# Two RoPE multiplications and one subtraction of the token mix moved from VectorE to GpSimd in an attention and channel-mix kernel

## The reference

```python
q = x @ Wq + bq;  k = x @ Wk + bk;  v = x @ Wv + bv      # split into 16 heads of 64
q = q * cos_pos + rotate_half_interleaved(q) * sin_pos   # RoPE
k = k * cos_pos + rotate_half_interleaved(k) * sin_pos
ctx = softmax(q @ k.T / 8) @ v
x = layernorm(x + ctx)

x_prev = x shifted by one token (zero at the first)
xr = mu_r * x + (1 - mu_r) * x_prev
xk = mu_k * x + (1 - mu_k) * x_prev
r = sigmoid(xr @ W_r.T)
out = layernorm(x + r * (square(relu(xk @ W_k.T)) @ W_v.T))
```

## Time and profile before

| | us |
|---|---|
| timed runs (2) | 4389.8 and 4480.0, median 4434.9 |
| profiled execution | 4356.1 |
| its span (slowest core, 7) | 4354.5 |
| spans of the eight cores | 4334.8 to 4354.5 |
| PE busy | 3102 (71%) |
| ACT busy | 2453 (56%) |
| DVE busy | 1065 (24%) |
| POOL busy | 245 (6%) |

### The profile page before, as it was taken

One profiled execution on the slowest core, in us unless ns is written; L12 is line 12 of the kernel. 1 busy time (PEld: TensorE's weight loads), 2 busy tenths in 40 slices (PEclk: granted clock), 3 DMA queues, 4 the chain that ended last, 5 costly groups with the idle time before them and its releaser, 6 DMA issues.

```text
span 4354.5 us, 53551 instructions; the slowest of 8 cores (4334.8 to 4354.5 us)
## 1 busy us (share of the span) xinstructions
PE 3102.2 (71%) x19520; PEld 1154.2 (27%) x19520; DVE 1065.3 (24%) x2489; ACT 2452.9 (56%) x2333; POOL 245.4 (6%) x260
## 2 busy tenths in 40 slices
PE   1555678878887888788788878887888787115554
PEld 1222222222222222322222222222223222002222
DVE  2222522212221221222122212212221000045553
ACT  0444057757775777577667757775776888001111
POOL 0111100010000001000100010010001000100000
PEclk9677899989998999899899989998998899557778
DMA  7342421111111110211011111102110000331110
GB/s 219 146 164 106 155 78 49 49 40 49 49 39 58 50 49 20 69 59 49 22 68 49 39 50 49 59 20 69 49 49 17 5 1 1 93 110 37 35 57 39
DMA packets 80352, 262.80 MB, mean 60 GB/s; under 512 B 6242, under 2 KB 40290, under 8 KB 61410
## 3 DMA queue, kind: packets, MB, share of 16 engines
q1 hardware_dynamic: 77282, 242.59, 16.5%
q0 software_dynamic: 2816, 16.78, 1.0%
HBM read 225.27 MB, written 34.08 MB: 60 GB/s over the span
## 4 chain that ended last, share of the span: by engine, by line
PE 44%; ACT 26%; issue 6%; DVE 6%; DMA 4%; DVEq 2%; POOL 1%; ACTq 0%; SPq 0%; POOLq 0%
ACT pt_sb L773 25%; PE ps_c L758 14%; PE ps_stB L747 6%; PE ps_b L560 5%; PE ps_b L599 5%; PE ps_stA L747 4%; PE ps_d L1261 1%; PE ps_d L1235 1%; PE ps_c L866 1%; PE ps_b L663 1%; DMA xf_b<-xT_spill 1%; DVE ctxT_f L791 1%; DVEq L168 1%; PE ps_b L921 1%; PE ps_c L798 1%
## 5 line engine op out<-in xcount | busy, mean ns | idle before, releaser
L773 ACT ACTIVATE pt_sb<-ps_stA,mhat_sb 128x1024 bf16<-128x1024 f32 x1024 | 1139.2, 1113 | 421.7 <-PE ps_c L758 258.0
L773 ACT ACTIVATE pt_sb<-ps_stB,mhat_sb 128x1024 bf16<-128x1024 f32 x1024 | 1139.9, 1113 | 270.2 <-PE ps_c L758 246.2
L758 PE MATMUL ps_c<-pt_sb,v_aug 128*65 128x512 bf16 x3968 | 1240.3, 394 | 0.0
L747 PE MATMUL ps_stB<-qT,kT 64*64 64x512 bf16 x4096 | 428.5, 404 | 186.1 <-ACT pt_sb L773 179.8
L747 PE MATMUL ps_stA<-qT,kT 64*64 64x512 bf16 x4096 | 430.6, 406 | 141.7 <-ACT pt_sb L773 126.5
L758 PEld LDWEIGHTS ps_c<-pt_sb,v_aug 128*65 128x65 bf16 x3968 | 279.5, 110 | 456.4 <-issue 456.4
L747 PEld LDWEIGHTS ps_stB<-qT,kT 64*64 64x64 bf16 x4096 | 136.4, 104 | 606.6 <-issue 600.8
L747 PEld LDWEIGHTS ps_stA<-qT,kT 64*64 64x64 bf16 x4096 | 135.9, 104 | 579.6 <-issue 572.4
L560 PE MATMUL ps_b<-xf_b,wkv_sb 128*128 128x512 bf16 x896 | 232.9, 407 | 51.1 <-DMA xf_b<-xT_spill 51.1
L654 POOL TENSOR_TENSOR ksq<-kT 128x512 bf16<-128x512 bf16 x112 | 115.4, 1037 | 2384.6 <-DVE kT L590 2370.5
L1156 PE MATMUL ps_t<-ident_sb,ctxg 128*128 128x128 f32 x136 | 33.0, 423 | 296.6 <-DVE ctxg L1146 296.6
(11 more groups left out here) (140 smaller groups left out, 2104.9 us busy)
## 6 DMA issues: line engine op xcount, KB each, us to landing
xf_b<-xT_spill SPq DMA_DIRECT2D x128, 1024.0 KB, 4.8
xst_f<-x_full SPq DMA_DIRECT2D x16, 2048.0 KB, 8.1
xT_spill<-xfT_st POOLq DMA_DIRECT2D x16, 1024.0 KB, 4.3
ctx_spill<-ctx_hp SPq DMA_DIRECT2D x8, 1088.0 KB, 5.8
xo_c<-x_own SPq DMA_DIRECT2D x17, 512.0 KB, 4.0
ctxg<-ctx_spill SPq DMA_DIRECT2D x17, 512.0 KB, 3.5
xst_f<-x_own SPq DMA_DIRECT2D x4, 2048.0 KB, 10.4
out<-xo_c SPq DMA_DIRECT2D x16, 512.0 KB, 2.6
```

Of the source, the lines that this page charges most:

```text
L747: r = e.matmul(ps_st[g].rearrange("p (b n) -> p b n", b=2) [half * 64:half * 64 + 64, h, 0:qn], kT2[buf][h * 64:h * 64 + 64, c * 128 + hal ...
L758: r = e.matmul(ps_c[h][0:65, 0:qn], v_aug[buf].rearrange("p (k x) -> p k x", k=KC) [:, cp, h * 65:h * 65 + 65], pt_sb[:, (cp % 4) * 1024 + ...
L773: sB.op("scalar", lambda e, g=g, c=c, hp=hp: e.activation(pt_sb[:, (c % 4) * 1024:(c % 4) * 1024 + 1024], ps_st[g][:, 0:1024], AF.Exp, bia ...
```

## The change

- Q RoPE: the two multiplications (`t1_sb`, `t2_sb`) go from DVE to POOL, without a drain between them. The addition into `qT2` stays on DVE as an operation of its own.
- K RoPE, in the fillers and in the prologue of head 0: the same with `bt1`, `bt2` and `kT2`. The list of a K/V tile in the fillers grows from ten items to eleven, so there are 194 items for 178.
- Token mix: mu * x + (1 - mu) * x_prev becomes x_prev + mu * (x - x_prev). POOL computes the difference of a chunk once (f32, into `tmp_f` or `tmp_g` in turn), DVE makes xr and xk from it by one scalar_tensor_tensor each. Sixteen tensor_scalar of a mix are gone from DVE and eight tensor_tensor come to POOL. xr and xk are now made chunk by chunk beside each other and no longer all of xr first.

```diff
-                def rope_q(e, pp=pp, hp=hp, qoff=qoff, qn=qn):
+                def rope_mul(e, pp=pp, qoff=qoff, qn=qn):
                     e.tensor_tensor(t1_sb[:, 0:qn], rq_sb[pp % 2][:, 0:qn],
                                     sinq_sb[:, qoff:qoff + qn], ALU.mult)
-                    e.drain()
-                    e.tensor_tensor(t2_sb[:, 0:qn], qpre[pp][:, 0:qn],
-                                    cosq_sb[:, qoff:qoff + qn], ALU.mult)
-                    e.drain()
-                    r = e.tensor_tensor(
-                        qT2[:, hp * FPAD + qoff:hp * FPAD + qoff + qn],
-                        t1_sb[:, 0:qn], t2_sb[:, 0:qn], ALU.add)
+                    r = e.tensor_tensor(t2_sb[:, 0:qn], qpre[pp][:, 0:qn],
+                                        cosq_sb[:, qoff:qoff + qn], ALU.mult)
                     return r
-                sA.op("vector", rope_q,
+                sA.op("gpsimd", rope_mul,
                       reads=[trk(f"rq{pp % 2}"), trk(f"qpre{pp}"), T["c_cosq"],
                              T["c_sinq"]],
-                      writes=[trk("qT2"), trk("t12")])
+                      writes=[trk("t12")])
+                sA.op("vector", lambda e, pp=pp, hp=hp, qoff=qoff, qn=qn:
+                      e.tensor_tensor(
+                          qT2[:, hp * FPAD + qoff:hp * FPAD + qoff + qn],
+                          t1_sb[:, 0:qn], t2_sb[:, 0:qn], ALU.add),
+                      reads=[trk("t12")], writes=[trk("qT2")])
...
-        def ropek(e, pp=pp, buf=buf, kt=kt):
+        def ropek_mul(e, pp=pp, kt=kt):
             e.tensor_tensor(bt1[:, :], rk_sb[pp][:, :],
                             sin2_sb[:, kt * 512:(kt + 1) * 512], ALU.mult)
-            e.drain()
-            e.tensor_tensor(bt2[:, :], kpre_sb[pp][:, :],
-                            cos2_sb[:, kt * 512:(kt + 1) * 512], ALU.mult)
-            e.drain()
-            r = e.tensor_tensor(kT2[buf][:, kt * 512:(kt + 1) * 512],
-                                bt1[:, :], bt2[:, :], ALU.add)
+            r = e.tensor_tensor(bt2[:, :], kpre_sb[pp][:, :],
+                                cos2_sb[:, kt * 512:(kt + 1) * 512], ALU.mult)
             return r
-        fl.append(lambda: sB.op("vector", ropek,
+        fl.append(lambda: sB.op("gpsimd", ropek_mul,
             reads=[trk(f"rk{pp}"), trk(f"kpre{pp}"), trk("cos2"), trk("sin2")],
-            writes=[trk(f"kT2_{buf}"), trk("btx")]))
+            writes=[trk("btx")]))
+        fl.append(lambda: sB.op("vector", lambda e, buf=buf, kt=kt:
+            e.tensor_tensor(kT2[buf][:, kt * 512:(kt + 1) * 512],
+                            bt1[:, :], bt2[:, :], ALU.add),
+            reads=[trk("btx")], writes=[trk(f"kT2_{buf}")]))
...
-            tags = ["dma", "kproj", "kevac", "rkmm", "rkevac", "rope",
+            tags = ["dma", "kproj", "kevac", "rkmm", "rkevac", "rope", "rope",
                     "vproj", "vevac", "vtr", "vsplit"]
...
-            def mix(e, doff=doff, dn=dn, tmp=tmp, mu=mu, om=om, dst=dst):
...
-                    e.tensor_scalar(tmp[:, 0:dn], cur, mu[:, cc:cc + 1],
-                                    None, ALU.mult)
-                    e.drain()
-                    r = e.scalar_tensor_tensor(
-                        dst[:, cc * 512:cc * 512 + dn], prv, om[:, cc:cc + 1],
-                        tmp[:, 0:dn], ALU.mult, ALU.add)
-                    e.drain()
...
+            sC.op("gpsimd", lambda e, dbuf=dbuf, dn=dn, cur=cur, prv=prv:
+                  e.tensor_tensor(dbuf[:, 0:dn], cur, prv, ALU.subtract),
+                  reads=xtags, writes=[trk(f"dmix{db}")])
+
+            def stt2(e, dbuf=dbuf, dn=dn, cc=cc, jb=jb, prv=prv):
+                e.scalar_tensor_tensor(
+                    xr_sb[jb][:, cc * 512:cc * 512 + dn], dbuf[:, 0:dn],
+                    mur_sb[:, cc:cc + 1], prv, ALU.mult, ALU.add)
+                r = e.scalar_tensor_tensor(
+                    xk_sb[jb][:, cc * 512:cc * 512 + dn], dbuf[:, 0:dn],
+                    muk_sb[:, cc:cc + 1], prv, ALU.mult, ALU.add)
+                return r
```

More of the change, by code:

```diff
@@ L962, in kv0_prologue, with ropek_mul @@
                 reads=[trk("b6")], writes=[trk(f"rk{pp}")])
-            def ropek(e, pp=pp, kt=kt):
+            def ropek_mul(e, pp=pp, kt=kt):
                 e.tensor_tensor(bt1[:, :], rk_sb[pp][:, :],
                                 sin2_sb[:, kt * 512:(kt + 1) * 512], ALU.mult)
-                e.drain()
-                e.tensor_tensor(bt2[:, :], kpre_sb[pp][:, :],
-                                cos2_sb[:, kt * 512:(kt + 1) * 512], ALU.mult)
-                e.drain()
-                r = e.tensor_tensor(kT2[0][:, kt * 512:(kt + 1) * 512],
-                                    bt1[:, :], bt2[:, :], ALU.add)
+                r = e.tensor_tensor(bt2[:, :], kpre_sb[pp][:, :],
+                                    cos2_sb[:, kt * 512:(kt + 1) * 512],
+                                    ALU.mult)
                 return r
-            sB.op("vector", ropek,
+            sB.op("gpsimd", ropek_mul,
                   reads=[trk(f"rk{pp}"), trk(f"kpre{pp}"), trk("cos2"),
                          trk("sin2")],
-                  writes=[trk("kT2_0"), trk("btx")])
+                  writes=[trk("btx")])
+            sB.op("vector", lambda e, kt=kt: e.tensor_tensor(
+                kT2[0][:, kt * 512:(kt + 1) * 512],
+                bt1[:, :], bt2[:, :], ALU.add),
+                reads=[trk("btx")], writes=[trk("kT2_0")])
             sB.op("gpsimd", lambda e, kt=kt: e.tensor_tensor(
@@ L1178, in emit_mix @@
         jb = j % 2
-        for eng, tmp, mu, om, dst, tag in (
-                ("vector", tmp_f, mur_sb, omr_sb, xr_sb[jb], f"xr{jb}"),
-                ("vector", tmp_g, muk_sb, omk_sb, xk_sb[jb], f"xk{jb}")):
-            def mix(e, doff=doff, dn=dn, tmp=tmp, mu=mu, om=om, dst=dst):
[L1183 to L1190, removed]
-                    e.tensor_scalar(tmp[:, 0:dn], cur, mu[:, cc:cc + 1],
-                                    None, ALU.mult)
-                    e.drain()
-                    r = e.scalar_tensor_tensor(
-                        dst[:, cc * 512:cc * 512 + dn], prv, om[:, cc:cc + 1],
-                        tmp[:, 0:dn], ALU.mult, ALU.add)
-                    e.drain()
-                return r
[L1199 to L1204, removed]
@@ new lines, in emit_mix @@
+        lo = (doff - 1) // 128
+        hi = (doff + dn - 1) // 128
+        xtags = [trk(f"x1T_{s}") for s in range(lo, hi + 1)]
+        for cc in range(NCC):
+            db = cc % 2
+            dbuf = (tmp_f, tmp_g)[db]
+            cur = x1T.rearrange("p (c t) -> p c t", c=NCC)[:, cc,
+                                                          doff:doff + dn]
+            prv = x1T.rearrange("p (c t) -> p c t", c=NCC)[:, cc,
+                                                          doff - 1:
+                                                          doff - 1 + dn]
+            sC.op("gpsimd", lambda e, dbuf=dbuf, dn=dn, cur=cur, prv=prv:
[8 more added lines that the diff above has]
+                    muk_sb[:, cc:cc + 1], prv, ALU.mult, ALU.add)
+                return r
+            sC.op("vector", stt2,
+                  reads=[trk(f"dmix{db}"), T["c_mur"], T["c_muk"]] + xtags,
+                  writes=[trk(f"xr{jb}"), trk(f"xk{jb}")])
```

## The result

The changed kernel is slower: the ratio of its time to that of the kernel before is 1.015, with a 95% interval of 1.010 to 1.020. On a time of 4356 us that is 66 us (44 to 88), where the sum had said 62.

A forecast was written before the change was run, and what follows sets the result against it. PE and ACT were busiest in attention; the Q stage was a serial chain with PE waiting at psa_u. 46 + 8 + 10 + 0 - 2 = +62 us, added to the fastest and median baselines, gave 4475 us midway, range 4405 to 4545.

The forecast's parts named there:

- the sum: Whole kernel: the predicted costs and gains of all parts added together, +62 us.
- the likeliest case: Whole kernel: time within 2% (88 us) of the kernel before, chance 0.78.
- Q RoPE, 46 us: Q stage, 40 tiles: longer DVE-POOL chain before PE's psa_u matmul, uncovered, costs 46 us, bounds 42 and 52.
- The clock, 8 us: Q stage: longer waits lower PE's granted clock, costing 8 us, bounds 0 and 39.
- Rival (a): Q stage: PE falls to the low clock throughout, 39 us for 8, sum +93, about 4506 us; chance 0.15.
- K/V of head 0, 10 us: First head's K/V stage, 16 tiles: DVE waits for POOL's multiplications, costing 10 us, bounds 5 and 16.
- Attention, 0 us: K RoPE under attention, 112 tiles: idle DVE and POOL time absorbs it, cost 0, bounds -10 and +20.
- the sign of being wrong: Changed profile: PE's wait growing by under 1 us, or attention moving by more than 20 us.
- rival (b): Attention: new filler spacing costs each projection burst 0.2 us more, 45 us, sum +107, about 4520 us; chance 0.08.
- The mix, -2 us: Token mix 0: subtractions on POOL and DVE work exclude each other, gaining 2 us, bounds -9 and +6.
- rival c: Token mix: POOL and DVE overlap freely, -9 us, sum +55, 4468 us; chance 0.05.
- Rival (d): Attention: DVE's shorter queue frees PE earlier, 112 us won, sum -50, about 4385 us; chance 0.02.

The follow-up runs named there:

- one_item: Changed kernel with the K RoPE's two POOL multiplications and DVE addition as one filler item, ten again; profiled time 4414.7 us, attention 3131.4 us.
- mix_dve: Kernel before with only the token mix's new formula, its difference also computed on DVE; profiled time 4394.1 us, first transposition to first projection of block C 81.7 us.

## Why the prediction was right, and where not

The direction and the likeliest case (within 2% of the kernel before, which had a chance of 0.78) came out as forecast, though the interval of 1.010 to 1.020 reaches to that bound. The agreement in the size is in part luck: +62 us in the sum, +66 by the ratio, but +80 between the fastest executions and on cores 0 to 3 of the two profiles, and the 18 us between are near the one wrong term. The time of 4475 us was put midway between two readings of a baseline that itself scattered from 4353 to 4592; the measured median of 4541 is 4 us inside the range given, and no term of the sum put it there. By its steps:

- **Q RoPE, 46 us.** Right: 45.5 us of wait, alone and in the whole change (43.0 on the 32 large tiles, for 42.6 in the sum, and 2.4 on the 8 small ones, for 3.7), and 13 us are left when PE has cover. One assumption in it was off. The multiplications were priced by the row of the squares, 1.035 us, and take 1.145; the hand-overs were in return shorter than put in, so the chain was 4.33 us for 4.24. The ratio of about 2 between the engines in the Trainium skill (GPSIMD Engine Reference, Engine selection), by which 33 us had been estimated, doesn't fit this trace: 1.145 against 0.425 us is 2.7.
- **The clock, 8 us.** Right in size: the stage grew by 6 to 10 us beside the wait. Over the Q projections on core 0 PE was busy for 183.0 us, for 172.1 before, at a mean granted clock of 0.68 for 0.70. Rival (a), 39 us, didn't come.
- **K/V of head 0, 10 us.** Right: 9.4. A round of DVE is 5.62 us (additions at 514.33 and 519.95) for 5.39 before; 5.75 had been predicted.
- **Attention, 0 us.** Wrong: 22 us, just above the upper bound of 20, which the prediction had also named as the sign of being wrong. The argument on POOL and DVE was right, as one_item shows: with 224 multiplications on POOL attention is as before. What failed was the last sentence of that step, that at 14.4 slots a tile for 14.2 "the items stay spread". The mean distance wasn't the question. The fillers are counted anew at each query tile's start, and the eleventh item moved the first projection of tiles 2 to 4 out of the pause at chunk 2. This is near rival (b), which had a cost by spacing, 45 us by a guess of 0.2 us a burst; it was given 0.08, and the mechanism in it, bursts meeting other PE work, is not the one found. Working out which item falls to which chunk from 0.703 and 0.766, as was done for the last items of each tile, would have shown it for the first ones.
- **The mix, -2 us.** -3.8 to -4.3. A subtraction beside DVE's work takes 1.60 us for 1.03, and the 9 us of free overlap (rival c) are not there. This is what the Trainium skill (SBUF — State Buffer, Who interferes with whom) says of such a pair of instructions, and the trace agrees. The term was some 2 us too small because six of the subtractions cost DVE 0.78 us each (1.53 for 0.75) and one 0.64, not 1.04. The squares of L1250 weren't held up (1.04 us each, for 1.07 before). The prediction credits the second engine with a gain that the formula alone gives: with everything on DVE it is the same.
- **Rival (d)** has no support: the wait list of attention has none of PE's K or V projections waiting for DVE, and freeing 0.8 us of DVE's time on each of 112 tiles moved nothing (one_item). Its 4385 us was counted from the median of 4434.9 and not from the base of the 4475.

## What to carry to other kernels

An operation moved to an idle engine is cheap where something else covers it and costs its full difference, hand-overs included, where the engine at the end has nothing else in its queue; so look first at what stands next in that queue, and move the waiting instruction later before moving the work. A list that is spread evenly over slots changes everywhere when it gets one item more: compare which item falls to which slot where the pipeline restarts, not the mean distance. Where DVE and POOL both read two tiles from SBUF, count their times as one engine's, as in the mix here (81.8 us with POOL, 81.7 without).

## What the runs showed of the hardware that was not expected

- A tensor_tensor of 128x512 bf16 on POOL takes 1034 to 1040 ns in the mean when both inputs are the same tile and 1145 to 1152 when they are two tiles; at 128x128 it is 398 or 399 and 425 to 427 ns. For f32 the subtraction of a tile and the same tile shifted by one column took 1.03 us.
- When a POOL and a DVE operation exclude each other, the later one ends 0.1 to 0.2 us earlier than the other's rest and its own time would make it. In the rows above POOL's subtraction of 3973.47 ends at 3975.07; DVE's operation of 3974.08 ends 0.54 us after that, where it takes 0.75 alone.
- The granted clock of PE can read 0.81 over whole stretches. A product with V (L758) took 446 ns in the mean in the stretch of mix_dve shown above and 392 ns from 2500 to 2580 us of the same execution.
